# A feed-forward block's folded weights made another way at the start of a one-core transformer kernel

## What is computed

```python
def butterfly(y, weights, dim):
    for stage in range(weights.shape[0]):          # 9 stages
        s = 2 ** stage
        nb = dim // (2 * s)
        yr = y.reshape(*lead, nb, 2, s)
        a, b = yr[..., 0, :], yr[..., 1, :]
        w = weights[stage].reshape(nb, s, 2, 2)
        na = w[..., 0, 0] * a + w[..., 0, 1] * b
        nb2 = w[..., 1, 0] * a + w[..., 1, 1] * b
        y = jnp.stack([na, nb2], axis=-2).reshape(*lead, dim)
    return y

def ffn(x):
    h = butterfly(x @ W_exp + b_exp, up_weights, 512)
    h = butterfly(gelu(h + up_bias), down_weights, 512)
    return h @ W_con + b_con + down_bias

x = x + 0.5 * ffn(layernorm(x))       # x is [1, 2048, 128]
x = x + attention(layernorm(x))       # 16 heads of 8; keys j with j % 4 == 0 or |i - j| <= 8
x = x + 0.5 * ffn(layernorm(x))
```

## Time and profile before

| what | value |
|---|---|
| median of three runs | 276.64 us |
| the profiled execution, its own time | 276.34 us |
| its span on the core | 274.4 us |
| PE busy | 251.5 us (92%) |
| ACT busy | 197.1 us (72%) |
| DVE busy | 126.6 us (46%) |
| POOL busy | 7.3 us (3%) |
| chain that ended last, by engine | PE 84%, ACT 8%, DVE 5% |

### The profile page before, as it was taken

How to read it: one execution, slowest core, us unless ns; L and a number is a source line. 1 busy time by engine, 2 the same in 40 slices (tenths; PEclk the granted TensorE clock), 3 DMA queues, 4 the chain that set the end, 5 groups by cost and what they waited for, 6 DMA issues and landing times.

```text
span 274.4 us, 6943 instructions
## 1 busy us (share of the span) xinstructions
PE 251.5 (92%) x2921; PEld 137.6 (50%) x2921; DVE 126.6 (46%) x408; ACT 197.1 (72%) x256; POOL 7.3 (3%) x12
## 2 busy tenths in 40 slices
PE   2697899999889999899999899999899999889995
PEld 0473675866434444345444354444454444476665
DVE  4986549897693033225234225324324520554311
ACT  0854347586759999887999887999878999624430
POOL 9100000000000000000000000000000000000000
PEclk9999999999999999999999999999999999999999
DMA  6940000486679541230331231233030000001111
GB/s 212 249 118 7 2 1 0 157 213 180 164 234 334 186 94 26 78 84 2 86 84 42 41 84 30 57 84 75 9 84 2 4 0 2 2 0 41 38 38 38
DMA packets 23887, 21.82 MB, mean 80 GB/s; under 512 B 4743, under 2 KB 22087, under 8 KB 23835
## 3 DMA queue, kind: packets, MB, share of 16 engines
q1 hardware_dynamic: 22742, 21.02, 28.4%
q10 hardware_dynamic: 1112, 0.34, 0.6%
HBM read 13.98 MB, written 7.56 MB: 79 GB/s over the span
## 4 chain that ended last, share of the span: by engine, by line
PE 84%; ACT 8%; DVE 5%; issue 1%; DMA 1%; DVEq 0%; ACTq 0%
PE ps L662 22%; PE ps L640 21%; PE ps L488 11%; PE ps L447 9%; PE ps L672 3%; PE ps L647 3%; PE ps L461 2%; PE ps L692 2%; ACT probs_all L863 2%; PE ps L680 1%; PE ps L473 1%; ACT gelu_h L757 1%; PE ps L523 1%; DMA resid<-L_attn_x 1%; DVE ctx_t L1148 1%
## 5 line engine op out<-in xcount | busy, mean ns | idle before, releaser
L859 ACT ACTIVATE probs_all<-ps 128x1024 f32<-128x1024 f32 x128 | 123.0, 1023 | 15.9 <-PE ps L640 12.3
L662 PE MATMUL ps<-probs_all,v_strided 128*32 128x256 f32 x1024 | 68.2, 384 | 0.2 <-ACT probs_all L859 0.2
L640 PE MATMUL ps<-q_slots,k_strided 75*128 75x512 bf16 x250 | 64.7, 381 | 2.9 <-ACT probs_all L863 2.5
L662 PEld LDWEIGHTS ps<-probs_all,v_strided 128*32 128x32 f32 x1024 | 27.1, 109 | 31.9 <-issue 10.8
L640 PEld LDWEIGHTS ps<-q_slots,k_strided 75*128 75x128 bf16 x250 | 20.4, 97 | 37.4 <-issue 11.7
L1135 DVE RECIPROCAL rden<-ps 128x16 f32<-128x16 f32 x16 | 4.1, 257 | 72.2 <-PE ps L680 72.2
L757 ACT ACTIVATE gelu_h<-ps,bias_up 128x512 f32<-128x512 f32 x32 | 21.8, 687 | 19.8 <-PE ps L447 19.7
L488 PE MATMUL ps<-down_folded,gelu_h 128*128 128x128 f32 x256 | 30.5, 277 | 2.7 <-ACT gelu_h L757 2.7
L488 PEld LDWEIGHTS ps<-down_folded,gelu_h 128*128 128x128 f32 x256 | 29.2, 192 | 5.2 <-ACT gelu_h L757 3.3
L447 PE MATMUL ps<-xnorm_t,up_folded 128*128 128x512 f32 x64 | 29.3, 600 | 1.7 <-ACT xnorm_t L748 1.0
L1161 DVE SCALAR_TENSOR_TENSOR probs_all<-probs_all,mask_k_sb 128x1024 f32<-128x1024 f32 x16 | 19.6, 1223 | 4.5 <-ACT probs_all L863 4.0
(11 more groups left out here) (116 smaller groups left out, 207.7 us busy)
## 6 DMA issues: line engine op xcount, KB each, us to landing
q_slots<-q_parts SPq DMA_DIRECT2D x16, 288.0 KB
k_local<-k_local_parts SPq DMA_DIRECT2D x48, 78.0 KB
q_parts<-prologue_or_parts SPq DMA_DIRECT2D x9, 384.0 KB, 4.0
k_strided<-k_strided_parts SPq DMA_DIRECT2D x12, 96.0 KB
q_parts<-last_parts SPq DMA_DIRECT2D x3, 384.0 KB, 5.1
k_local_parts<-prologue_or_parts SPq DMA_DIRECT2D x3, 288.0 KB, 5.1
resid<-L_attn_x SPq DMA_DIRECT2D x1, 768.0 KB, 10.2
out<-resid SPq DMA_DIRECT2D x3, 256.0 KB, 2.3
```

The lines of the kernel that those rows point to most:

```text
L640: mm = pe.matmul(PS[:, b0 + i, :], KS[:, ch, G * g + h, :], QS[:, g, h, :], start=True, stop=True)
L662: mm = pe.matmul(PS[VC * h:VC * (h + 1), 6 + n % 2, 0:QB // 2], VS[:, ch, at:at + VC], probs, start=(ch == 0 and r == 0), stop=False, skip ...
L859: act.activation(PE_[:, ch // 2, 2 * m:2 * m + 2, ch % 2, :], PS[:, b0:b0 + 2, :], ACT.Exp).then_inc(p_ready, 1)
```

## The change

- **Up side.** DVE's levels stop at 512 columns, and the last of these takes its factors from PSUM (a spread row, no longer loaded for all partitions). PE multiplies `W_exp` with these 512 columns, four 128x128 products. The last two stages are then done by DVE on the product: 1,024 columns multiplied (`UP7`), 512 added (`UP7S`), 1,024 multiplied (`UP8`), and twice 256 added straight into `UPW`. ACT's copy is gone; a new ACT copy of 1,024 columns puts stage 7's factors into SBUF (`SEVENS`).
- **Down side.** ACT scales 128x128 chunks of `W_con` 8 times (`CON8`), DVE adds, multiplies 1,024 columns and adds (`CON4`, `CONM`, `CONS`), PE makes 4 products and not 16. All of it from `CON4` on stands behind the up side on DVE, and PE's products stand behind `ffn_up(0)`. ACT's copy to `DNW` is behind block 0's gelu.
- **Far weights.** One operand of 8 rows (`FAR`) and six selectors of 8x128 (`SEL`); PE spreads with 6 matmuls (`spread`), each of 8 rows from partition 0, five at the start and one later.
- **Loads.** The near weights shrink from 1,032 to 520 columns per side; the up weights go first, then `W_exp` on SP's queue.
- **Layer norm.** `layernorm(TB, NT - TB)` in the head, 12 tiles, becomes `layernorm(TB, TB)`, 4 tiles. The other 8 tiles are taken in block 0's turn, between `normalize(0, XN2)` and `ffn_ahead(1)`.
- **POOL** waits for `qx_ready` of block 0 before its two large memsets.

The diff (eight columns of indentation taken off; left out are the semaphores' declarations, the host's layout of the weights and the selector table):

```diff
@@ -82,10 +82,11 @@
 UPW = sb("up_folded", [P, HID])
-PRO = sb("prologue_or_parts", [P, 2 * NEAR + 2 * HID])
+PRO = sb("prologue_or_parts", [P, 6 * QB])
 WUP = PRO[:, 0:NEAR]
 WDN = PRO[:, NEAR:2 * NEAR]
-WUF = PRO[:, 2 * NEAR:2 * NEAR + HID]
+FAR = PRO[0:8, 2 * NEAR:2 * NEAR + HID]
+SEL = PRO[0:8, 2 * NEAR + 2 * HID:2 * NEAR + 2 * HID + 6 * P].rearrange("p (n k) -> p n k", n=6)
 WT = PRO[:, 2 * NEAR + HID:2 * NEAR + 2 * HID].rearrange("p (c d) -> p c d", c=NC)
...
@@ -247,9 +247,11 @@
-UPB = [WUP[:, 2 * MIX:2 * MIX + 2 * NC]] + levels(4 * NC, 0)
-WCM = ARENA[:, 2 * NC * HID:3 * NC * HID].rearrange("p (o j d) -> p o j d", o=NC, j=NC)
-DNB = [WDN[:, 2 * MIX:2 * MIX + 2 * NC]] + levels(4 * NC, 3 * NC * HID)[:STAGES - 3]
+UPB = [WUP[:, 2 * MIX:2 * MIX + 2 * NC]] + levels(4 * NC, 0)[:STAGES - 3]
+DNB = [WDN[:, 2 * MIX:2 * MIX + 2 * NC]] + levels(4 * NC, 2 * HID)[:STAGES - 3]
+UP7, UP7S, UP8 = ARENA[:, 2048:3072], ARENA[:, 3072:3584], ARENA[:, 3584:4608]
+SEVENS = ARENA[:, 7680:8704]
+CON8, CON4, CONM, CONS = ARENA[:, 4608:5632], ARENA[:, 5632:6144], ARENA[:, 6144:7168], ARENA[:, 7168:7680]
 def pairs_of(b):
...
@@ -269,8 +271,9 @@
     sp.dma_start(X[:, 0:TB, :], x_t[:, 0:TB, :]).then_inc(ld_x[0], 16)
+    sp.dma_start(WUP[:, :], up_near).then_inc(ld_up, 16)
+    sp.dma_start(WT[:, :, :], w_exp_t.rearrange("(c p) d -> p c d", p=P)).then_inc(ld_wt, 16)
     sp.dma_start(WDN[:, :], dn_w).then_inc(ld_dn, 16)
-    sp.dma_start(WUP[:, :], up_near).then_inc(ld_up, 16)
     sp.dma_start(WCON[:, :, :], w_con.rearrange("(c p) d -> p c d", p=P)).then_inc(ld_wc, 16)
...
@@ -413,6 +416,7 @@
     pool.memset(XTL[:, PADK + 3 * S // 4:XLW], 0.0).then_inc(xtl_zero, 1)
+    pool.wait_ge(qx_ready, TB)
     pool.memset(VS[:, :, :], 0.0).then_inc(v_zero, 1)
...
@@ -440,42 +444,43 @@
         for c in chunks:
+            if b == 0:
+                pe.wait_ge(upw_sb, c // 2 + 1)
             if 2 <= b < NB and c == 2:
                 pe.wait_ge(v_ready, 3 * (b - 1))
             if b % NB:
                 pe.wait_ge(g_ready, NC * (b - 1) + c + 1)
             pe.matmul(PS[:, 1 + c, :], UPW[:, c * P:(c + 1) * P], XT[:, :], start=True, stop=True).then_inc(h_ps, 1)
-    pe.wait_ge(one_set, 1)
-    pe.wait_ge(ld_uf, 16 * NC)
-    for r in range(NC):
-        mm = pe.matmul(PS[:, (6, 7, 4, 5)[r], :], ONE[32 * r:32 * r + 1, :], WUF[32 * r:32 * r + 1, :], start=True, stop=True)
-    mm.then_inc(wbc, 1)
+    def spread(i, bank):
+        pe.matmul(PS[:, bank, :], SEL[:, i, :], FAR[:, :], start=True, stop=True).then_inc(wbc, 1)
+    pe.wait_ge(ld_uf, 16 * 2)
+    spread(0, 3)
+    spread(1, 6)
+    spread(2, 7)
+    spread(3, 4)
+    spread(4, 5)
     pe.wait_ge(ld_id, 16)
     transpose_block(0)
-    pe.wait_ge(dn_fold, STAGES - 3)
-    for j in range(NC):
-        pe.wait_ge(wc_mix, j + 1)
-        for o in range(NC):
-            mm = pe.matmul(PS[:, 2, j * P:(j + 1) * P], DNB[-1][:, j * P:(j + 1) * P], WCM[:, o, j, :],
-                           start=(o == 0), stop=(o == NC - 1))
-    mm.then_inc(dnw_ps, 1)
+    pe.wait_ge(ld_wt, 16)
+    pe.wait_ge(up_fold, STAGES - 3)
+    for c in range(NC):
+        mm = pe.matmul(PS[:, 1, c * P:(c + 1) * P], WT[:, c, :], UPB[STAGES - 3][:, c * P:(c + 1) * P], start=True, stop=True)
+    mm.then_inc(upw_ps, 1)
     pe.wait_ge(ld_bx, 16 * 2)
-    pe.wait_ge(up_fold, STAGES - 3)
     for j in range(NC):
         mm = pe.matmul(PS[:, 3, j:j + 1], UPB[STAGES - 3][:, j * P:(j + 1) * P], BEX[:, j:j + 1], start=True, stop=True)
     mm.then_inc(bup_ps, 1)
-    pe.wait_ge(ld_wt, 16)
-    for c in range(NC):
-        pe.wait_ge(up_fold, STAGES - 2 + c + 1)
-        mm = pe.matmul(PS[:, 1, :], WT[:, c, :], UPB[-1][:, c * HID:(c + 1) * HID], start=(c == 0), stop=(c == NC - 1))
-    mm.then_inc(upw_ps, 1)
-    pe.wait_ge(upw_sb, 1)
+    pe.wait_ge(sev_sb, 1)
+    spread(5, 6)
     pe.wait_ge(bup_set, 1)
     ffn_up(0)
+    pe.wait_ge(dn_fold, STAGES - 3)
+    pe.wait_ge(wc_mix, 1)
+    for j in range(NC):
+        mm = pe.matmul(PS[:, 7, j * P:(j + 1) * P], DNB[-1][:, j * P:(j + 1) * P], CONS[:, j * P:(j + 1) * P], start=True, stop=True)
+    mm.then_inc(dnw_ps, 1)
...
@@ -733,13 +738,12 @@
-    for r in range(NC):
-        act.dma_start(WUF[32 * r:32 * r + 1, :], up_far[r:r + 1, :]).then_inc(ld_uf, 16)
+    act.dma_start(FAR[:, :], up_far).then_inc(ld_uf, 16)
+    act.dma_start(SEL[:, :, :], far_sel).then_inc(ld_uf, 16)
+    act.dma_start(UN[:, :], unity[None, :].partition_broadcast(P).rearrange("p a b -> p (a b)")).then_inc(ld_un, 16)
     act.dma_start(ID[:, :], ident).then_inc(ld_id, 16)
     act.dma_start(BEX[:, :], b_exp).then_inc(ld_bx, 16)
     act.dma_start(UBC[:, :], up_b).then_inc(ld_bx, 16)
-    act.dma_start(WT[:, :, :], w_exp_t.rearrange("(c p) d -> p c d", p=P)).then_inc(ld_wt, 16)
-    act.dma_start(UN[:, :], unity[None, :].partition_broadcast(P).rearrange("p a b -> p (a b)")).then_inc(ld_un, 16)
...
@@ -809,27 +813,29 @@
-    act.wait_ge(xb_ready, 1)
-    for t in range(TB):
-        act.activation(XN[:, 0, t, :], X[:, t, :], ACT.Identity, bias=XB[:, t:t + 1], scale=RS[:, t:t + 1]).then_inc(xn_ready, 1)
-    act.wait_ge(dn_mix, 1)
-    act.wait_ge(ld_wc, 16)
-    for j in range(NC):
-        for o in range(NC):
-            ins = act.activation(WCM[:, o, j, :], WCON[:, o, :], ACT.Copy, scale=KDN[:, o, j:j + 1])
-        ins.then_inc(wc_mix, 1)
     act.wait_ge(ld_un, 16)
     act.activation(SG[:, 0:1], UN[:, :], ACT.Exp, scale=-1.0).then_inc(sig, 1)
     act.wait_ge(sig, 1)
     act.activation(SG[:, 3:4], SG[:, 0:1], ACT.Gelu).then_inc(table, 1)
-    act.wait_ge(dnw_ps, 1)
-    act.activation(DNW[:, :, :].rearrange("p c d -> p (c d)"), PS[:, 2, :], ACT.Copy).then_inc(dnw_sb, 1)
+    act.wait_ge(wbc, 3)
+    act.activation(SEVENS, PS[:, 6:8, :].rearrange("p a b -> p (a b)"), ACT.Copy).then_inc(sev_sb, 1)
+    act.wait_ge(xb_ready, 1)
+    for t in range(TB):
+        act.activation(XN[:, 0, t, :], X[:, t, :], ACT.Identity, bias=XB[:, t:t + 1], scale=RS[:, t:t + 1]).then_inc(xn_ready, 1)
+    act.wait_ge(ld_dn, 16)
+    act.wait_ge(ld_wc, 16)
+    for h in range(2):
+        for m in range(NC):
+            n = h * NC + m
+            ins = act.activation(CON8[:, n * P:(n + 1) * P], WCON[:, 2 * h + m // 2, :], ACT.Copy, scale=WDN[:, n:n + 1])
+    ins.then_inc(wc_far, 1)
     operand(0)
-    act.wait_ge(upw_ps, 1)
-    act.activation(UPW[:, :], PS[:, 1, :], ACT.Copy).then_inc(upw_sb, 1)
     for b in range(NB + 1):
         if b < NB:
             gelu(b)
+        if b == 0:
+            act.wait_ge(dnw_ps, 1)
+            act.activation(DNW[:, :, :].rearrange("p c d -> p (c d)"), PS[:, 7, :], ACT.Copy).then_inc(dnw_sb, 1)
         if b == NB - 1:
...
@@ -948,32 +953,43 @@
-    dve.wait_ge(ld_dn, 16)
-    mix(KDN, WDN, dn_mix)
-    at = 2 * MIX + 2 * NC
-    for st in range(1, STAGES - 2):
-        n = NC * 2 ** (st + 1)
-        o = DNB[st - 1][:, :, None].to_broadcast([P, n // 2, 2])
-        w = WDN[:, at:at + n].rearrange("p (m h) -> p m h", h=2)
-        dve.tensor_tensor(DNB[st].rearrange("p (m h) -> p m h", h=2), o, w, ALU.mult).then_inc(dn_fold, 1)
-        dve.wait_ge(dn_fold, st)
-        at += n
     dve.wait_ge(ld_up, 16)
     mix(KUP, WUP, up_mix)
     at = 2 * MIX + 2 * NC
-    for st in range(1, STAGES - 2):
+    for st in range(1, STAGES - 3):
         n = NC * 2 ** (st + 1)
         w = WUP[:, at:at + n].rearrange("p (m h s) -> p m h s", m=NC, h=2)
         widen(UPB[st], UPB[st - 1], w, NC, up_fold)
         dve.wait_ge(up_fold, st)
         at += n
     dve.wait_ge(wbc, 1)
-    widen(UPB[STAGES - 2], UPB[STAGES - 3], PS[:, 6:8, :].rearrange("p a (m h s) -> p (a m) h s", m=2, h=2), NC, up_fold)
-    dve.wait_ge(up_fold, STAGES - 2)
-    for c in range(NC):
-        widen(UPB[STAGES - 1][:, c * HID:(c + 1) * HID], UPB[STAGES - 2][:, c * HID // 2:(c + 1) * HID // 2],
-              PS[:, 4 + c // 2, :].rearrange("p (m h s) -> p m h s", m=1, h=2), 1, up_fold)
+    widen(UPB[STAGES - 3], UPB[STAGES - 4], PS[:, 3, :].rearrange("p (m h s) -> p m h s", m=NC, h=2), NC, up_fold)
+    def pairwise(new, old, w, done):
+        o = old[:, :, None].to_broadcast([P, old.shape[-1], 2])
+        dve.tensor_tensor(new.rearrange("p (m h) -> p m h", h=2), o, w.rearrange("p (m h) -> p m h", h=2), ALU.mult).then_inc(done, 1)
+    dve.wait_ge(ld_dn, 16)
+    at = 2 * MIX + 2 * NC
+    for st in range(1, STAGES - 3):
+        n = NC * 2 ** (st + 1)
+        pairwise(DNB[st], DNB[st - 1], WDN[:, at:at + n], dn_fold)
+        dve.wait_ge(dn_fold, st)
+        at += n
+    dve.wait_ge(upw_ps, 1)
+    dve.wait_ge(sev_sb, 1)
+    widen(UP7, PS[:, 1, :], SEVENS.rearrange("p (m h s) -> p m h s", m=NC, h=2), NC, fold_step)
+    dve.wait_ge(fold_step, 1)
+    u7 = UP7.rearrange("p (a b s) -> p a b s", a=2, b=2)
+    dve.tensor_tensor(UP7S.rearrange("p (a s) -> p a s", a=2), u7[:, :, 0], u7[:, :, 1], ALU.add).then_inc(fold_step, 1)
+    dve.wait_ge(fold_step, 2)
+    dve.wait_ge(wbc, 5)
```

(21 more changed lines are left out.)

32 lines of the change are left out of this document (19 added, 13 removed).

## The result

The changed kernel takes 290.53 us (median of 4 runs, 290.40 to 292.82), the kernel before 276.62 (4 runs): ratio 1.0489, 95% interval [1.0439, 1.0540]. The forecast was 282.7, with a range of 278.0 to 285.2: the sign was right, the size was not. The profiled execution took 290.40 us, its span 288.6 (before 274.4).

The account below looks back on a forecast made before the run. The prediction took PE to bound the kernel (84% of the chain), with DVE on the path ahead of block 2's transposes. Its terms, -3.7 + 0.9 + 7.5 + 1.4 = +6.1 us, gave 282.7 us, range 278.0 to 285.2.

Parts of the forecast that it names:

- Term 1: Head, up side: with the new spreads and products `ffn_up(0)` starts at 18.05 and not 21.75, -3.7 us.
- everything at the lower level: Late bound of the head: spreads and all behind them at the lower clock, `ffn_up(0)` starting at 21.5, -0.2 us.
- Term 2: Down side behind `ffn_up(0)`: PE products, ACT's copy and hand-overs take 1.77 us until `ffn_down(0)`, today 0.87; +0.9 us.
- Term 3: Moved tiles ahead of block 2's `xnorm`: POOL's memsets hold DVE's `var_eps`, +7.5 us; 4.15 without the hold.
- Term 4: PE idles about 8 us before block 2's transposes, then 2.9 us of work runs at the lower clock: +1.4 us.
- the forecast's bound of 2.0: Upper bound on the cost of lower clock behind PE's idle stretch, 2.0 us; the lower bound was 0.
- I see nothing later that isn't released by PE's own order: After 45 us: all losses lie before that point and nothing is given back later.
- No hold: Rival at DVE's `var_eps`: moved memsets run beside DVE, +4.15 us, 278.0 us and up to 1.4 more; chance 0.12.
- faster: Rival in head and DVE: DVE not held, `ffn_up(0)` before 16.7, 275.8 us at the early bound; chance 0.07.
- delay lost later: Rival: later work waits elsewhere, say at attention's loads, so a delay of 6 us disappears there; chance 0.03.
- Hold there, clock kept: Rival behind PE's idle stretch: memsets hold DVE, but PE keeps the upper clock over 8 us idle; 281.3 us, chance 0.20.
- the forecast's own bound of 286.8: Upper end of the hold case with the bounds of head and clock, 279.1 to 286.8 us.

Follow-up runs that it names:

- b1_tiles_moved: Kernel before, with only the second eight tiles' layer norm moved behind block 0's query and key norm; 282.56 to 282.99 us, ratio 1.0183.
- a2_tiles_back: Changed kernel with the statistics of blocks 2 and 3 back in the head, POOL's wait kept; 284.97 to 290.95 us, ratio 1.0277.
- b2_tiles_pool_moved: Kernel before, with the eight tiles' layer norm moved and POOL's memsets waiting for `qx_ready`, head unchanged; median 285.44 us, ratio 1.0274.
- d1_after_twenty: Changed kernel plus twenty bf16 matmuls of 26 rows by 26 columns at PE's start; 285.84 to 287.75 us, ratio 1.0359.
- f3_after_rows128: Changed kernel, both moves kept, with 128-row spreads, two 512-column matmuls ahead of `ffn_up(0)` and sixteen small ones at the start; median 283.45 us, ratio 1.0212.
- c1_rows128: Changed kernel with tile and POOL moves undone, spreads reading 128 rows, 120 zeroed by DVE ahead of the loads; 277.29 to 278.93 and 282.37 to 284.48 us.
- e2_rows128_warm: Both moves undone, 128-row spreads, matmuls ahead of `ffn_up(0)`, small ones at the start, plus six 128-row matmuls ahead of the spreads; median 275.85 us, ratio 0.9937.
- e1_rows128_filled: Changed kernel, both moves undone, with 128-row spreads, two 512-column matmuls ahead of `ffn_up(0)`, sixteen small ones at the start; median 275.69 us, ratio 0.9948.
- a3_both_back: Changed kernel with both moves undone: 12 tiles' statistics in the head, POOL's memsets from block 0's reciprocal root there; 278.54, 283.24, 283.5 and 285.08 us.

## Why the prediction was wrong

- *Term 1, the head, -3.7: this step failed.* It took "the first 2.9 us at the lower level", read off, where PE worked on 128 rows, and gave spreads of 8 rows the same rise. They never got it: the level was low from 4.12 to about 25. The 2.9 us were also one execution's: in `b1_tiles_moved` the same 32 matmuls took 6.67 us, all at the lower level, and 128-row spreads of 7.44 and 6.47 us mean a rise some 6 and 4 us after their start (an estimate, from 0.89 and 0.46 us an instruction). Some parts of the sum were right: one instruction behind another (0.89 us each, 0.925 in the forecast) and L905 in the head at 0.17. `SEVENS`, copied at 9.64 (forecast 9.3), was right by luck: the loads came 0.9 us earlier than forecast, which hid the missing rise. But the fifth spread, the products and `ffn_up(0)` all ran at half speed: -1.34 at the start of `ffn_up(0)` and +2.26 in its length, so `ffn_down(0)` came 4.4 us later than forecast. The bound "everything at the lower level" (21.5) held its start, and had no price for its length.
- *Term 2, +0.9:* +0.70, from 0.87 us behind `ffn_up(0)` to 1.57. Right.
- *Term 3, +7.5:* +7.58. The hold of 3.4 us, its end with POOL's memset, 8 us of idleness: right; removing the wait removed the hold. The rule that the prediction took from the Trainium skill (SBUF — State Buffer, "SBUF: two separate sides") fits `a2_tiles_back` too, where the memset held the larger `xnorm` steps of the same kind.
- *Term 4, +1.4:* +1.62. Right here, but with luck in the size: behind idle stretches of the same 8.2 us it was 1.28 in `b2_tiles_pool_moved` and in `d1_after_twenty`, and 2.56 in `f3_after_rows128`, beyond the forecast's bound of 2.0.
- *"I see nothing later that isn't released by PE's own order": this failed too.* PE's own code was late at the branch: 2.17 us and 1.24 of lower clock behind, in the profiled run, 3.4 us together. The forecast counted what PE executes and not where it lies; that fewer instructions stand ahead of a branch had no term and no rival.
- *The rivals.* "No hold" and "faster" fell with L911's 3.47 us; "delay lost later" fell, it grew. "Hold there, clock kept" fell with the products of 4.83 us.
- *The range* put its upper end at 285.2, short of the forecast's own bound of 286.8. The chain above gives 283.45 without the two losses, inside it; with the head's loss alone the runs gave 286.2, and with the branch's alone it would be 283.45 + 3.4 = 286.9 (worked out, not run). Either loss puts the time outside the range.

## What to carry to other kernels

A TensorE stage that is busy is not yet one at the upper clock: a stretch of matmuls over a few rows can leave everything behind it at half speed, so cost it at the lower level, with the work that follows, unless a row of the same shape shows otherwise. Where a kernel branches, compare the time at which PE is due there with the last instruction packet in the trace, before and after; removing instructions ahead of it can cost more than they took. When work is moved behind a wait, look at which engine's long memset or copy it will meet at the new place: the row of the old place has the price.

## What the runs showed that I had not expected

- Spreads over 8 rows, without a pause for 8.9 us and with other work up to 19.3 (4.25 us of it over 128 rows), raised nothing; the same over 128 rows, 120 of them zeros, raised the clock inside 7.44 us (6.47 in `f3_after_rows128`). What exactly has to be busy isn't shown.
- Once up, the clock fell behind an idle stretch of 2.87 us (`c1_rows128`), and behind one of 1.78 (`e2_rows128_warm`), but not behind one of 1.79 (`e1_rows128_filled`). In `a3_both_back` it fell at 72 us behind stretches of 0.59 and 1.07.
- A 16 KB packet of instructions arriving late went with 2.1 to 3.6 us of idleness at a branch, and moving the prefetch hint one block earlier made no difference (290.4 to 293.5).
- Twenty bf16 matmuls of 26 columns took 0.68 us, ten fp32 ones of 32 columns 4.47.
